# A two-layer perceiver block: the first layer's tail done one sequence at a time, its last part beside the next layer's attention

## The reference

```python
x = x + _L0_xattn_ref(_layernorm(x), ctx, ctx, mask, ...)
x = x + _L0_attn_ref(_layernorm(x), ...)     # the mixing block
x = x + _L0_ffn_ref(_layernorm(x), ...)
x = x + _L1_xattn_ref(_layernorm(x), ctx, ctx, mask1, ...)
x = x + _L1_attn_ref(_layernorm(x), ...)
x = x + _L1_ffn_ref(_layernorm(x), ...)

# mixing block, for h = rmsnorm(x)
gate, val = split(linear(h, in_w, in_b)); gate = sigmoid(gate)
a = linear(dwconv(val, 4 taps) @ A @ Bm, ha_w, ha_b)
b = linear(linear(silu(dwconv(val, 9 taps)), pw_w, pw_b), hb_w, hb_b)
y = linear(gate * linear(concat(a, b), fuse_w, fuse_b), out_w, out_b)
# feed-forward
h = gelu(bitlinear(layernorm(x), w1, b1))
h = bitlinear(layernorm(h), w2, b2)          # bitlinear: each row scaled, rounded, clipped
# second cross-attention
att = softmax(wq(x) @ wk(ctx).T / 16 + mask1) @ wv(ctx)
```

## Time and profile before

| | us |
|---|---|
| three runs | 1048.58, 1050.47, 1052.31 |
| median | 1050.47 |
| the profiled execution's own time | 1047.13 |
| its span | 1045.3 |
| TensorE busy | 916.5 (88%) |
| VectorE busy | 601.9 (58%) |
| ScalarE busy | 487.4 (47%) |
| GpSimd busy | 78.2 (7%) |

### The profile page before, as it was taken

One profiled execution on the slowest core, in us unless ns is written; L12 is line 12 of the kernel. 1 busy time (PEld: TensorE's weight loads), 2 busy tenths in 40 slices (PEclk: granted clock), 3 DMA queues, 4 the chain that ended last, 5 costly groups with the idle time before them and its releaser, 6 DMA issues.

```text
span 1045.3 us, 14987 instructions
## 1 busy us (share of the span) xinstructions
PE 916.5 (88%) x5913; PEld 527.1 (50%) x5914; DVE 601.9 (58%) x1064; ACT 487.4 (47%) x955; POOL 78.2 (7%) x87
## 2 busy tenths in 40 slices
PE   6379799999999999999988995059999989999878
PEld 2246444444555555555445543034755854566656
DVE  3647777777874458888443836953233127288240
ACT  1623366777764567777884411322220210677201
POOL 2312011111000000000002000300000007000000
PEclk9979899999999999999998998669999989999979
DMA  9845733454322212226028006032625350000000
GB/s 357 220 90 158 250 104 104 139 151 132 87 69 65 61 32 67 74 74 195 15 103 296 1 1 241 0 149 93 241 81 211 112 161 0 1 1 1 1 0 21
DMA packets 65555, 108.67 MB, mean 104 GB/s; under 512 B 6854, under 2 KB 40390, under 8 KB 63302
## 3 DMA queue, kind: packets, MB, share of 16 engines
q1 hardware_dynamic: 63276, 100.35, 30.3%
q10 hardware_dynamic: 2208, 7.34, 1.8%
HBM read 93.77 MB, written 13.89 MB: 103 GB/s over the span
## 4 chain that ended last, share of the span: by engine, by line
PE 79%; DVE 9%; ACT 6%; issue 3%; DMA 2%; SPq 0%; POOL 0%; ACTq 0%; DVEq 0%
PE psum L1575 12%; PE psum L1557 10%; PE psum L1528 10%; PE psum L1512 5%; PE psum L1860 5%; PE psum L1831 5%; PE psum L1502 5%; PE psum L1684 4%; PE psum L1889 4%; PE psum L1697 4%; PE psum L1921 3%; ACT arena L715 2%; PE psum L1935 2%; DVE arena L991 1%; PE psum L2021 1%
## 5 line engine op out<-in xcount | busy, mean ns | idle before, releaser
L991 DVE TENSOR_REDUCE arena<-psum 128x1 f32<-128x1024 f32 x256 | 301.7, 1219 | 121.2 <-PE psum L1528 121.1
L715 ACT ACTIVATE arena<-psum 128x512 f32<-128x512 f32 x512 | 264.7, 604 | 63.6 <-PE psum L1557 62.5
L1557 PE MATMUL psum<-arena 99*128 99x256 bf16 x1024 | 161.3, 275 | 8.4 <-ACT arena L715 4.8
L1528 PE MATMUL psum<-arena 96*128 96x512 bf16 x512 | 152.9, 382 | 6.5 <-DVE arena L991 5.5
L1575 PE MATMUL psum<-arena 128*32 128x256 f32 x2048 | 136.8, 385 | 0.0
L1557 PEld LDWEIGHTS psum<-arena 99*128 99x128 bf16 x1024 | 80.4, 98 | 107.1 <-ACT arena L715 50.6
L1575 PEld LDWEIGHTS psum<-arena 128*32 128x32 f32 x2048 | 53.5, 109 | 75.4 <-ACT arena L715 36.9
L1502 PE MATMUL psum<-arena 128*128 128x512 f32 x128 | 64.3, 630 | 24.1 <-DMA arena<-wkT 9.0
L1512 PE MATMUL psum<-arena 128*128 128x256 f32 x256 | 62.9, 389 | 1.3 <-ACT arena L693 1.3
L1528 PEld LDWEIGHTS psum<-arena 96*128 96x128 bf16 x512 | 49.4, 99 | 25.9 <-DVE arena L991 12.9
L607 POOL TENSOR_TENSOR arena<-arena 128x512 bf16<-128x512 f32 x34 | 40.8, 1199 | 213.4 <-DVE arena L977 206.7
(11 more groups left out here) (234 smaller groups left out, 989.0 us busy)
## 6 DMA issues: line engine op xcount, KB each, us to landing
arena<-kparts SPq DMA_DIRECT2D x192, 128.0 KB, 3.1
kparts<-arena SPq DMA_DIRECT2D x32, 384.0 KB, 3.4
arena<-ctxT SPq DMA_DIRECT2D x18, 512.0 KB, 5.1
arena<-ctxT SPq DMA_DIRECT2D x2, 4096.0 KB, 12.9
arena<-ctx SPq DMA_DIRECT2D x2, 4096.0 KB, 14.3
arena<-mask SPq DMA_DIRECT2D x8, 1024.0 KB, 6.8
arena<-mask ACTq DMA_DIRECT2D x4, 1024.0 KB, 12.2
arena<-w1e SPq DMA_DIRECT2D x2, 2048.0 KB, 10.2
```

Source lines behind the costliest of these rows:

```text
L715: nc.scalar.activation(PR[step % 4][:, pair * CH:(pair + 1) * CH], ring_bank(slot), ACT.Exp)\
L991: nc.vector.tensor_reduce(MX[g % 2][:, col:col + 1], unit_banks(n).rearrange("p b n -> p (b n)"), AX.X, ALU.max).then_inc(s_maxed, 1)
L1528: last = nc.tensor.matmul(out, q, KST[g % 2][0:ROWS, j, at], start=True, stop=not masked, skip_group_check=True)
L1557: last = nc.tensor.matmul(ring_heads(slot)[:, u, :], KST[gg % 2][0:KROWS, j, kc * P:(kc + 1) * P], QST[0:KROWS, G * g + j, b * S:(b + 1) * S],
```

## The change

Mixing block and feed-forward layer of the first layer are done for the first sequence, then for the second, on half-width instructions (256 tokens). The second sequence's up projection comes among the key scores of window 0; its quantising, down projection and queries come among windows 0 and 1, which belong to the first sequence. All score units of windows 2 and 3 then go ahead of both their weighings. The ring of score banks has three in place of four, since the others are lent to these pieces. Six buffers move or get one buffer for each tile, the arena grows from 53,120 to 56,960 words, and a reserve for dynamic DMAs is set to 1,024 bytes.

```diff
-        arena = ctx.enter_context(nc.sbuf_tensor("arena", [P, 53120], F32))
+        arena = ctx.enter_context(nc.sbuf_tensor("arena", [P, 56960], F32))
...
+        UH = [f32(at, 1024).rearrange("p (t f) -> p t f", t=1) for at in (24576, 25600, 53120, 54144)]
+        QH = [b16(at, 1024) for at in (26624, 27136, 55168, 55680)]
+        UP_BANKS = ((7, 0, 2, 1), (7, 3, 7, 3))
+        DOWN_BANKS = (5, 6, 3, 7)
...
-            load_mask(0)
-            load_mask(1)
-            sp.wait_ge(on["x_ready"], 3 * TT)
-            load(CTXT[1], by_part_of(t["ctxT"][1]), "ctxt_loaded1")
-            for n in range(2, 4):
+            for n in range(5):
                 load_mask(n)
             sp.wait_ge(on["e_scores"], 16)
             load(CTXK[1], t["ctx"][1].rearrange("(k p) c -> p k c", p=P), "ctxk_loaded1")
-            for n in range(4, 8):
+            load_mask(5)
+            sp.wait_ge(on["x_ready"], 3 * TT)
+            for n in range(4):
+                at = slice(n * 1024, (n + 1) * 1024)
+                load(CTXT[1][:, :, at], by_part_of(t["ctxT"][1])[:, :, at], f"ctxt_loaded{n + 1}")
+            for n in range(6, 8):
                 load_mask(n)
...
+            for b in range(B):
+                pool.wait_ge(on["d_centred"], b + 1)
+                odd = UH[2 * b + 1][:, 0, :]
+                nc.gpsimd.tensor_tensor(odd, odd, row("g2"), ALU.mult).then_inc(on["d_gained"], 1)
```

ScalarE's new order from the input projection's copies on:

```diff
+            copy_in(0)
+            copy_in(1)
+            sigmoids(0, 0)
+            copy_hbpw(0)
+            copy_hbpw(1)
...
+            sigmoids(0, 1)
+            act.wait_ge(on["c_hbpw_copied"], IT + 2)
+            copy_hb(0)
...
+            copy_a(0)
+            copy_ha(0)
+            sigmoids(1, 0)
+            copy_a(1)
+            sigmoids(1, 1)
+            copy_ha(1)
+            root(0, 2)
+            copy_hb(1)
...
+            copy_quantised(0)
+            gelus(0)
+            root(0, 2)
+            centre_odd(0)
+            copy_hidden(0)
+            copy_hidden(1)
+            root(2, 4)
+            root(0, 2)
+            copy_turned_half(0)
+            copy_queries(0)
+            copy_folded(0)
+            copy_quantised(1)
+            gelus(1)
+            key_exps(0)
+            root(2, 4)
+            centre_odd(1)
+            copy_exps(0)
+            copy_hidden(2)
+            key_exps(1)
+            copy_hidden(3)
+            root(2, 4)
+            copy_exps(1)
+            copy_turned_half(1)
+            copy_queries(1)
+            copy_folded(1)
+            for w in range(2, 4):
+                key_exps(w)
+                copy_exps(w)
```

VectorE, behind the first sequence's addition of the mixed rows and within windows 0 and 1:

```diff
+            for n in range(8):
+                mask_unit(0, n)
+                if 2 <= n < 6:
+                    hidden(1, n - 2)
...
+            for n in range(8):
+                mask_unit(1, n)
+                if n == 0:
+                    hidden_stats(1, 3)
+                    aggregate(2, 2, 4)
+                    ask_root(2, 4)
+                if n == 4:
+                    take_root(2, 4)
+                    turn_means(1)
+                if n == 5:
+                    gain(2)
+                if n == 6:
+                    shift(2)
+            bias_exps(1)
+            find_scale(2)
+            copy_exps(0, 1)
+            quantise_hidden(2)
+            for n in range(3, 8, 2):
+                copy_exps(0, n)
+            shift(3)
+            find_scale(3)
+            quantise_hidden(3)
+            add_down(1)
```

TensorE, in the attention:

```diff
-                    if 8 * w + n >= 4:
-                        pe.wait_ge(on["e_masked"], 8 * w + n - 3)
+                if unit >= 3:
+                    pe.wait_ge(on["e_masked"], unit - 2)
...
+            for n in range(8):
+                key_scores(0, n)
+                if 1 <= n < 5:
...
+                    project_up(1, n - 1)
+            for n in range(8):
+                key_scores(1, n)
+            turn_exps(0)
+            pe.wait_ge(on["d_hidden"], 8)
+            turn_hidden(2)
+            weigh_context(0, 0, 8)
+            project_down(2)
+            weigh_context(0, 8, 16)
+            turn_hidden(3)
...
+            turn_exps(1)
+            weigh_context(1, 0, 8)
+            pe.wait_ge(on["x_ready"], 3 * TT)
+            turn_half(HLE, 1, 2 * TT)
...
+            for w in range(2, 4):
+                for n in range(8):
+                    key_scores(w, n)
+            for w in range(2, 4):
+                turn_exps(w)
+                weigh_context(w)
...
-    nc = bacc.Bacc("TRN2", target_bir_lowering=False, num_devices=1)
+    nc = bacc.Bacc("TRN2", target_bir_lowering=False, num_devices=1, dynamic_dma_scratch_size=1024)
```

More of the change, by code:

```diff
@@ L843, in _ @@
[L843 to L850 removed]
+            copy_hb(0)
+            act.wait_ge(on["c_a"], 1)
@@ new lines, in add_down_bias, with turn_means @@
+            def add_down_bias(b):
+                done()
+                for i in (2 * b, 2 * b + 1):
+                    mark(nc.vector.tensor_tensor(X[:, i, :], X[:, i, :], row("w2b"), ALU.add))
+            def turn_means(b):
+                two = slice(2 * b, 2 * b + 2)
+                nc.vector.scalar_tensor_tensor(out=NEGM[:, two], in0=mean[:, two, 0], scalar=-1.0,
+                                               in1=SD[:, 4 + 2 * b:6 + 2 * b],
+                                               op0=ALU.mult, op1=ALU.mult).then_inc(on["d_means"], 1)
```

727 lines of the change are left out of this document (432 added, 295 removed).

## The result

The changed kernel takes **1025.74 us** (median of 4 runs, 1022.15 to 1026.64); the one before 1051.39 (4 runs, 1048.58 to 1053.05). The ratio is **0.9765, 95% interval 0.9735 to 0.9794**. The forecast was 1024.4, range 1012 to 1040. The profiled execution of after took 1022.15 with a span of 1020.4; the sum had given 1021.0 for it.

What follows compares the result with a forecast made beforehand. TensorE was taken as the bound (79% of the wait chain), idle some 46 us behind VectorE's serial chain. -42.2 + 16.1 = -26.1 us gave 1021.0 from the profiled execution, 1024.4 against the median; range 1012 to 1040.

Steps and rivals of the forecast that it cites:

- Mixing block: From 574.35, one sequence at a time: ends at 641.0, 4 us later than before, first up projection included.
- VectorE's convolution: Mixing block: 30.1 us for 24.0, some 5 us of sigmoid waits, ends at 613.8 before fuse; priced at nothing.
- Feed-forward layer of the first sequence: From the up projection's end at 634.6 to key scores at 669.0, which start 42.2 us earlier than 711.25.
- What rides along: Second sequence's feed-forward during attention: 9.6 us on TensorE, 4.7 late exponential copies, 1.8 clock drop; 16.1 us given back.
- Ring of three banks, table loads, mask and context loads: Attention: three score banks, five more ScalarE table loads, reordered mask and context loads all covered; priced at nothing.
- GpSimd's port: Feed-forward multiplication on GpSimd beside VectorE: charged nothing; under the skill's shared-port rule 1.2 us worse.
- Outside: Before 574.35 and behind 843.40: nothing reordered, no change counted.
- The signs: Trace marks: first key score near 669, TensorE idle some 15 us in 641 to 659, exponential copies over 9 to 10.
- The clock stays low: Rival: four mixing-block pauses each drop the clock, 7.2 us more, 1032; chance 0.15.
- Not covered: Rival: in-order queues put the second feed-forward's VectorE work on the attention's path, 16.4 us more, 1041; chance 0.08.
- More comes back: Rival: pieces overlap better than in order, up to 8.3 us and some hand-overs gained, 1012; chance 0.03.
- Slower: Outcome slower than before, chance 0.06; rival on record: small DMA reserve throttles transfers, 3% to 4% slower.

Runs made afterwards that it cites:

- filler_more: combined plus 16 more useless matmuls in six short TensorE waits in code the change did not touch; 1005.75 us, 0.9579 against the kernel before.
- all_joined: filler_more with tile 3's multiplication back on GpSimd and VectorE's gain and shift of tile 2 behind the first exponentials' copies; 1005.37 us, ratio 0.9579.
- no_gpsimd_gain: Changed kernel with feed-forward tile 3 centred and multiplied by VectorE, not ScalarE and GpSimd; 1019.53 us, 0.9733 against the kernel before.
- ffn_before: Changed kernel with the second sequence's feed-forward layer wholly ahead of the first key score; 1034.36 us, 0.9862 against the kernel before.
- reserve_only: Kernel before with only the 1,024-byte dynamic DMA reserve and the larger arena; 1048.97 us, ratio 0.9980.
- copies_first: Changed kernel with VectorE copying the first turned exponentials before tile 2's scale search and quantising; 1023.07 us, 0.9761 against the kernel before.
- order_two: Changed kernel with the edits of copies_first and no_gpsimd_gain, plus VectorE's root and centring between its later copies; 1019.67 us, 0.9693 against the kernel before.
- combined: order_two plus the 23 useless matmuls of filler_half; 1012.08 us, 0.9630 against the kernel before; run again, 1012.15 us, 0.9647.
- filler_half: Changed kernel plus 23 useless matmuls where TensorE waits for the first sequence's quantising; 1018.33 us, 0.9690 against the kernel before.

## Why the prediction was right, by its own steps

Times of after are less 1.44 here, the later start of the front.

- **Mixing block.** Input projections and folded weights took 22.67 where 64 and 32 records at 0.221 give 21.2: a clock drop that I had not placed there. The drop of 1.8 that I had placed at hb (from the earlier trace rows) did not come: 3.69 us. The two cancel, and hb ends at 603.1 for a forecast of 603.0; that was luck as to the place. In every trace but those of filler_more and all_joined there is one drop here, at one of the two places: in no_gpsimd_gain the 96 took 20.99 and hb 5.37. From there fuse ends at 614.5 (614.6), the first output projection at 622.8 (622.6), the up projection at 634.2 (634.6), the second output projection, the 3.72 us at 638.52, at 640.8 (641.0).
- **VectorE's convolution.** 16 passes took 6.42, so 0.401 each (forecast 0.418); it waited 3.74, 0.78 and 0.41 for sigmoids, 4.9 in all (forecast 5), and ended at 613.1 (613.8), ahead of fuse. Priced at nothing, it cost nothing.
- **Feed-forward layer of the first sequence.** Tiles ready at 647.1 and 651.8 (647.4, 652.3), down projection to 655.9 (656.3), first key score at 667.4 (669.0). Of the 1.6 too many 0.4 were there by the end of the down projection; 1.1 are in the copy behind the queries, the folding and the biases, 3.4 us where I had 4.5, with the clock back at 1.00 from 665. Up to the first key score it came out at -43.9 for -42.2.
- **What rides along.** +14.5 for +16.1. Up projections 1.7 (1.7); transposes and down projections 2.9 (2.8); the second half's turn, queries and biases 4.7 (5.0). turn_exps(0) cost 5.4 more than before. I had 4.7 for it and 1.8 for the clock, 6.5 in all. The size was near, but the parts were not: I gave VectorE 0.5 us of lateness, and it came 1.4 later still, because its shift stood beside GpSimd's pass (no_gpsimd_gain). Against that, the quantising between the copies cost TensorE 1.0 (the second eight records start 2.45 behind the first, for 1.44 before) and not 1.86, and the clock drop (0.50 from 703 to 709) 0.9 of the 1.8; the rest of it fell on time in which TensorE waited anyway. My 5.5 that become 9.7 also held 0.6 that the 1.75 and the 1.86 do not give.
- **Ring of three banks, table loads, mask and context loads.** No wait of a key score for a mask in the rows; windows 2 and 3 run as one block of 27.71 us, which is 2 x 13.9; the third block starts at 749.49 with no wait for the context. Nothing, as priced.
- **GpSimd's port.** I charged nothing and said that the trace could not separate row and rule. It is the place where the reasoning was wrong. The 2.95 of the earlier trace rows was no length of the pass alone: alone it takes 2.35, and the rest was waiting for passes of VectorE. The first sequence hardly suffered: GpSimd's pass did start behind the shift, but was over at 645.2 (I had 645.3), and VectorE's first quantising pass took 0.96 for 0.75. The second did, by 1.4 us, at a place that I had not thought of.
- **Outside.** I had the rest unchanged. It was, in its order; it was 4.5 us longer in the profiled execution, the clock's doing at least behind 815, and this hid that the two stages were 3.3 better than forecast (29.4 for 26.1). That the sum comes within 1.2 us of the profiled execution (1021.0 for 1022.15) is in this part luck; the mechanism and each stage's size were right.
- **The signs.** Two did not come as I gave them: TensorE was idle for 12 us between 641 and 659, not 15, and the copies of the first turned exponentials spread over 6.9 us (703.03 to 709.97), not 9 to 10, since much of the lateness lay ahead of the first. One sign of being wrong came true, "if the stretch before 574.35 changes at all": it was 1.4 us longer. But it is 573.8 to 577.3 in kernels that are alike there, so it was no sign of anything.

The rivals. "The clock stays low" did not come in the mixing block, where only the one drop was seen; the low stretch of 20 us at 644 was in the forecast. "Not covered" is refuted by ffn_before: uncovered, the layer costs 14.9 more by the trace, for my 16.4, and in after it did not. "More comes back" came in the two stages, by 3.3 us of its 12, and not in the time. "Slower" is refuted by reserve_only.

## What to carry to other kernels

Where two halves of a batch are independent, find the stage in which the bounding engine waits for a serial chain, and put the other half's work there: here, by the stage lengths, half of the gain came from running the chain once per half beside matmuls of the other (by difference), half from riding in the next layer's attention (ffn_before). What rides along costs its own matmuls, which are easy to add up, and its places in the in-order queues of the other engines: look for each short pass on which the bounding engine waits every microsecond, and put no long pass ahead of it; moving one such block only helps if the next such place is looked at too (copies_first). Then look at the clock of every stretch and not at its mean.

## What the runs showed of the hardware that I had not expected

**The clock's falls behind short waits, and fillers.** In nearly every trace of kernels without fillers at these places TensorE's granted clock fell to its lower level for some microseconds at up to five places: about 562 to 570, 576 to 580 or at hb, 644 to 665, 702 to 710, and behind 817. Each lies behind a pause or thin matmuls, and which of two neighbouring places is hit changes from one profile to the next. Matmuls without a use in pauses of 6.3, 1.1, 0.8, 1.1 and 2.7 us kept it at the full level from 644 to 664 in all seven profiles that have them. The fall at 702 to 710 was gone where VectorE's order left no long wait there (order_two and all that build on it). With 16 more in pauses of 0.7 to 2.8 us the falls at 576 and 817 were gone as well in both kernels that have them; the one near 564, behind matmuls with one row, stayed, only shorter. From combined to filler_more the ratio fell by 0.5 to 0.7 of a percentage point, with no overlap of the single times. From after to filler_half it fell by 0.75, but the two stages show only 1.9 us of that. The Trainium skill, in TensorE: Matmul & The Clock Gate, "What's actually happening", says that the low clock is the default state and that activity releases it; these runs agree, with 0.50 behind the pauses and 1.00 where they were filled. No run here shows what the fillers cost in power.

**VectorE and GpSimd exclude each other for a whole pass.** VectorE's shift of 1,024 columns with two inputs in SBUF: 1.28 us alone, 2.65 when issued while GpSimd multiplies. GpSimd's multiplication: 2.35 alone, 3.36 to 3.41 when issued while such a pass of VectorE runs. The mask pass at 696.78, which reads one input from PSUM, took its usual 0.69 beside it. Both waits are about what was left of the other's pass: in after GpSimd waited 1.05 when 1.18 were left of VectorE's, VectorE 1.37 when 1.57 were left of GpSimd's. That is as the Trainium skill has it in SBUF — State Buffer, "SBUF: two separate sides": whichever starts first has the shared pair for its whole instruction. The same section also names passes of VectorE in its fast modes. The trace of before fits that: of its passes with one SBUF input, issued beside GpSimd's three, one took 2.71 for 0.69 and the next 2.44 for 0.43, 2.0 us more each:

```profile
670.93 2.44 DVE L1281 TENSOR_SCALAR arena<-arena 128x1024 bf16<-128x1024 bf16 x1
...
677.81 0.43 DVE L1281 TENSOR_SCALAR arena<-arena 128x1024 bf16<-128x1024 bf16 x1
```

No experiment here set out to test it.
